# A decoder layer pair on one core: the last output product of the cross attention in two steps, the order of normalisations moved at three places, and the second block's rows loaded ahead of the second expert's weights

## The reference, cut to what matters

```python
x = x + L0_attn(layernorm(x))      # 32 heads of 64, 8 key heads, sinks
x = x + L0_xattn(layernorm(x), mask, ctx)   # 32 heads of width 16, 375 context rows
x = x + L0_ffn(layernorm(x))       # router, 8 experts, 2 per row: gelu(x Wg) * (x Wu), then Wd
x = x + L1_attn(layernorm(x))      # 16 heads of 128, low-rank keys and values
x = x + L1_xattn(layernorm(x), ctx, mask)
x = x + L1_ffn(layernorm(x))       # amplitude and phase, two rounds of products and layernorms
```

## Time and profile before

| | |
|---|---|
| three executions | 1752.63, 1756.43, 1756.64 us; median 1756.43 |
| the profiled execution, its own time | 1756.78 us |
| its span (first to last instruction) | 1754.5 us |
| TensorE busy / weight loads | 1700.0 us (97%) / 1137.6 us (65%) |
| VectorE, ScalarE, GpSimd busy | 986.4, 548.0, 458.5 us |
| mean granted TensorE clock | 0.996 |
| DMA | 172.26 MB, mean 98 GB/s |

### The profile page before, as it was taken

The page is one execution under the profiler, slowest core; times in us unless marked ns, Lnnn a source line. Parts: engine busy times, 40 slices in busy tenths (PEclk is TensorE's granted clock), DMA queues, the critical chain, the costliest instruction groups (busy, mean ns, idle before and its releaser), DMA issues.

```text
span 1754.5 us, 32913 instructions
## 1 busy us (share of the span) xinstructions
PE 1700.0 (97%) x13868; PEld 1137.6 (65%) x13868; DVE 986.4 (56%) x1901; ACT 548.0 (31%) x1515; POOL 458.5 (26%) x549
## 2 busy tenths in 40 slices
PE   7999999999999999999999999998999999999998
PEld 6876666657666666666546888877677775444444
DVE  3765556437777777677743111116554555664987
ACT  0343333524444444445410111110422222333411
POOL 2532323512222213222113000005231210002676
PEclk9999999999999999999989999999999999999999
DMA  9100012000000000000147988866000033752101
GB/s 394 49 1 1 1 43 73 1 27 19 13 8 19 4 17 20 8 13 1 67 171 294 347 334 335 335 231 229 2 1 1 1 137 129 241 189 84 29 14 42
DMA packets 31987, 172.26 MB, mean 98 GB/s; under 512 B 4024, under 2 KB 4024, under 8 KB 18176
## 3 DMA queue, kind: packets, MB, share of 16 engines
q1 hardware_dynamic: 29600, 162.82, 24.9%
q0 software_dynamic: 2240, 7.34, 1.2%
HBM read 155.46 MB, written 16.52 MB: 98 GB/s over the span
## 4 chain that ended last, share of the span: by engine, by line
PE 86%; DVE 10%; POOL 1%; issue 1%; ACT 1%; DMA 1%; POOLq 0%; DVEq 0%; ACTq 0%
PE PS L1312 9%; PE PS L1080 7%; PE PS L1131 6%; PE PS L1381 5%; PE PS L1459 5%; PE PS L1169 5%; PE PS L1490 4%; PE PS L1321 4%; PE PS L1426 4%; PE PS L1192 3%; PE PS L1209 3%; PE PS L1477 3%; PE PS L1139 3%; PE PS L1156 2%; PE PS L1161 2%; DVE R L1618 2%
## 5 line engine op out<-in xcount | busy, mean ns | idle before, releaser
L1312 PEld LDWEIGHTS PS<-R,W 128*128 128x128 f32 x1344 | 153.2, 192 | 11.7 <-issue 11.7
L1312 PE MATMUL PS<-R,W 128*128 128x128 f32 x1344 | 153.6, 275 | 2.2 <-DVE R L1811 2.2
L1634 DVE TENSOR_REDUCE nmw<-PS 112x2 f32<-112x750 f32 x128 | 114.1, 934 | 42.5 <-PE PS L1192 42.5
L2251 POOL TENSOR_TENSOR rstd<-veps,mhalf 128x1 f32<-128x1 f32 (+1 forms) x71 | 53.8, 757 | 307.2 <-DVE veps L1520 284.0
L1080 PE MATMUL PS<-xT,W 128*128 128x224 f32 x640 | 127.8, 360 | 1.0 <-ACT xT L2041 0.7
L1080 PEld LDWEIGHTS PS<-xT,W 128*128 128x128 f32 x640 | 122.2, 194 | 9.9 <-issue 7.6
L1818 DVE TENSOR_TENSOR R<-R,PS 128x512 f32<-128x512 f32 x21 | 14.5, 688 | 199.1 <-PE PS L1312 199.1
L1459 PE MATMUL PS<-W 128*128 128x512 f32 x256 | 119.8, 611 | 0.9 <-ACT R L2109 0.9
L2109 ACT ACTIVATE R<-PS 125x672 f32<-125x672 f32 x128 | 86.6, 730 | 85.8 <-PE PS L1209 85.8
L2277 POOL TENSOR_TENSOR R<-R 128x224 f32<-128x224 f32 x80 | 52.8, 661 | 223.4 <-DVE R L1545 116.6
L1381 PE MATMUL PS<-xT,W 128*128 128x224 f32 x512 | 101.9, 359 | 2.5 <-DVE R L1545 2.2
(11 more groups left out here) (306 smaller groups left out, 3325.3 us busy)
## 6 DMA issues: line engine op xcount, KB each, us to landing
W<-in_we SPq DMA_DIRECT2D x63, 1024.0 KB, 8.0
R<-in_ctxT SPq DMA_DIRECT2D x12, 750.0 KB, 7.3
W<-in_entwT SPq DMA_DIRECT2D x8, 1024.0 KB, 7.0
W<-in_entpw SPq DMA_DIRECT2D x8, 1024.0 KB, 8.3
R<-in_ctx SPq DMA_DIRECT2D x8, 750.0 KB
xs_rows<-in_x SPq DMA_DIRECT2D x3, 1792.0 KB, 36.1
R<-xs_rows SPq DMA_DIRECT2D x21, 256.0 KB, 8.3
ys_rows<-R SPq DMA_DIRECT2D x21, 256.0 KB, 8.5
```

Of the source, the lines that this page charges most:

```text
L1312: o = e.matmul(PS[:, m, c * 128:(c + 1) * 128], gate_up(j % 3, k, off + c * 128), BT[:, j % 2, k, :], start=k == 0, stop=k == 3)
L1634: e.tensor_reduce(nmw[0:S, par, :].rearrange("p (r f) -> p r f", r=4)[:, r:r + 2, 16 - 16 * par], PS[0:S, r:r + 2, 0:SC], AX.X, ALU.max, n ...
```

## The change

Some dozen of the 2210 steps change their place; no step is added, taken away or given another PSUM bank. The output product ("xw", 6) is cut in two on TensorE: three of its four products ask for less than the last.

```diff
@@ -382,7 +382,8 @@
                     k = fill.index(need)
                     mine = [f for f in fill[:k + 1] if f[0] == need[0] or {f[0], need[0]} in ({"ck", "ck1"}, {"pj", "rt"})]
                     out += [take(f) for f in mine]
-        out += runs[n]
+        final = n == 16 * NBATCH - 1
+        out += runs[n][:-1] + [("mt", *pieces_of(n // 4), 1)] + runs[n][-1:] if final else runs[n]
         due += unit * SHARE[n % 4]
         some = []
         while True:
@@ -390,11 +391,11 @@
             if not free or not (due > cost(free[0]) / 2 or n == 16 * NBATCH - 1 or n % 4 in MUST and not some):
                 break
             some.append(take(free[0]))
-        if n % 4 == 3:
+        if n % 4 == 3 and not final:
             some.insert(1, ("mt", *pieces_of(n // 4), 1))
         out += some
     h = part(range(5))
-    at_end = {("xk", 7, 3, 1): h[:1], ("xcv", 7, 3, 1): h[1:4], ("xd", 7, 3): [("scale", 2, 5)], ("xw", 6): h[4:5] + [("turn", 2, 5)] + h[5:6] + [("route", 1)]}
+    at_end = {("xk", 7, 3, 1): h[:1], ("xcv", 7, 3, 1): h[1:2], ("xw", 6): [("scale", 2, 5)] + h[2:3] + [("turn", 2, 5)] + h[3:4] + [("route", 1)]}
     for s in itertools.chain(*runs[16 * NBATCH:]):
         out += [s] + at_end.get(s, [])
     return out
@@ -402,9 +403,9 @@
 
 def experts():
 
-    out = [("load", "front", 3), ("load", "we", 0), ("load", "w1s", 0), ("scale", 2, 6), ("turn", 2, 6), ("route", 2), ("lt",)] + part([3]) + [("rank",)]
-    out += part(range(4, FRONT)) + [("ea", 0, k) for k in range(FRONT)] + [("put", t) for t in range(NT)]
-    out += [("load", "experts", 0), ("load", "rows", 0), ("load", "we", 1), ("load", "rows", 1), ("load", "rows", 2), ("load", "we", 2)]
+    out = [("load", "front", 3), ("load", "we", 0), ("load", "w1s", 0), ("scale", 2, 6), ("turn", 2, 6), ("route", 2), ("lt",)] + part([2]) + [("rank",)]
+    out += part(range(3, FRONT)) + [("ea", 0, k) for k in range(FRONT)] + [("put", t) for t in range(NT)]
+    out += [("load", "experts", 0), ("load", "rows", 0), ("load", "rows", 1), ("load", "we", 1), ("load", "rows", 2), ("load", "we", 2)]
     out += [("bt", 0), ("pc", 0), ("pc", 2)]
     for j in range(NBLK + 1):
         if j < NBLK:
@@ -458,6 +459,8 @@
 
 def pace1(step):
 
+    if step[0] in ("stats", "scale"):
+        return 0.0
     return float(step[0] == "d1") if step[0] in ("p1", "s1", "c1", "v1", "d1", "w1") else cost(step)
 
 
@@ -539,7 +542,7 @@
             if u == 0:
                 out += nxt[:4]
                 nxt = nxt[4:]
-            nxt = norms(0, bs) + nxt[:4] + turns(0, bs) + nxt[4:]
+            nxt = [("stats", 0, b) for b in bs] + nxt[:1] + [("scale", 0, bs[0])] + nxt[1:2] + [("scale", 0, b) for b in bs[1:]] + nxt[2:4] + turns(0, bs) + nxt[4:]
         else:
             nxt = norms(1, (0, 1)) + nxt[:4] + turns(1, (0, 1)) + norms(1, (2,)) + nxt[4:] + turns(1, (2,))
         if u == NU - 2:
@@ -563,7 +566,7 @@
         nxt = project1(u + 1) if u + 1 < NU else []
         if u + 2 < NU:
             bs = range(2 * u + 4, min(2 * u + 6, NT))
-            nxt = norms(3, bs) * (u > 0) + nxt[:5] + turns(3, bs) + nxt[5:]
+            nxt = nxt[:5] + turns(3, bs) + nxt[5:]
         if u + 1 < NU:
             nxt += [("bo1", t) for t in range(0 if u == 0 else 2 * u + 2, min(2 * u + 4, NT))]
         if u == NU - 1:
@@ -577,7 +580,11 @@
         if u == 0:
             second = attend1(1)
             out += norms(3, (4, 5)) + once[4:10] + second + once[10:]
-        out += spread([s for n in range(2 * (u == 0), 4) for s in attend1(4 * u + n)], nxt, pace1)
+        steps = [s for n in range(2 * (u == 0), 4) for s in attend1(4 * u + n)]
+        if u and u + 2 < NU:
+            k = steps.index(("c1", u, 0, 1)) + 1
+            steps[k:k] = norms(3, bs)
+        out += spread(steps, nxt, pace1)
     out += [("load", "c5", 0), ("load", "c5", 1), ("mu",)]
     out += attend1(4 * NU) + attend1(4 * NU + 1)
     out += [("load", "ent", 1, 0), ("load", "ent", 1, 3), ("load", "rows2a", 0)]
@@ -1260,9 +1267,12 @@
                     return
                 m = bank(("xw", t))
                 w.wait_ge(*at("d_q3", "wx"))
-                for b in (t, t + 1):
-                    w.wait_ge(*at("oxt", (b, 3)))
-                xw_part(t, m, range(4)).then_inc(*up("attended", ("xw", t)))
+                w.wait_ge(*at("oxt", (t, 3)))
+                if t == NT - 1:
+                    w.wait_ge(*at("oxt", (t + 1, 2)))
+                    xw_part(t, m, range(3))
+                w.wait_ge(*at("oxt", (t + 1, 3)))
+                xw_part(t, m, range(3 * (t == NT - 1), 4)).then_inc(*up("attended", ("xw", t)))
 
             def route(part):
                 m = bank(("route", part))
@@ -2326,9 +2336,9 @@
 
             def lt():
                 w.wait_ge(*at("var", 0))
+                e.tensor_tensor(rt[:, 8, 8:8 + NT], rt[:, 8, 0:NT], mhalf[:, 0:NT], ALU.pow).then_inc(*up("rms", 0))
                 for n in range(8):
                     e.memset(rsl(rt, 9)[:, :, n:n + 1], 8.0 - n).then_inc(*up("rank", n))
-                e.tensor_tensor(rt[:, 8, 8:8 + NT], rt[:, 8, 0:NT], mhalf[:, 0:NT], ALU.pow).then_inc(*up("rms", 0))
 
             def put(b):
                 w.wait_ge(*at("slot_no", 0))
```

## The result

The changed kernel takes **1745.57 us** (median of 4 executions, 1744.57 to 1749.1) against 1756.54 (4 executions, 1752.63 to 1757.42): a ratio of 0.9945, 95% interval 0.9925 to 0.9966. Later executions put the size in proportion: over all 15 of the changed kernel, these four among them, the median is 1747.05 (1743.9 to 1749.82), over 79 of the kernel before 1756.48, so about 9.4 us. Three later executions, of two of the experiments and of the kernel before, took 2439, 6053 and 7702 us and are left out of every figure.

What follows compares the result with a forecast made beforehand. The prediction took TensorE's own stream to bound the kernel (busy 1700.0 of 1754.5 us). Its terms, -1.30 - 0.82 - 3.05 - 2.37 + 0.1 = -7.4 us, took 1756.78 to 1749.3, range 1747.0 to 1753.6.

Steps and rivals of the forecast that it cites:

- scale(0,4) and (0,5) later: Layer 0: VectorE's copy comes before two scalings, so TensorE's value product no longer waits for it; gain 1.30 us.
- scale(0,6) frees no wait of TensorE: Layer 0: moving this third scaling later was to gain nothing, no TensorE wait being found there.
- cost nothing: Layer 0: the scalings' new places between rotations were to cost 0; 0.5 us for GpSimd contention went into the range.
- Gain 0.82: End of the cross attention: TensorE no longer waits for VectorE's addition of maxima, queued behind a denominator; 0.82 us.
- gain 3.05: End of the cross attention: with less idle time the clock stays up, so 6.1 us of work takes half the time.
- rival A: The clock falls all the same, or in another place: gain 4.4 us, time 1752.4; chance 0.2.
- xw(6): Output product split in two, less filler ahead: TensorE waits 0.1 us for the last piece, range 0 to 0.5.
- Rows 1: Expert stage: loading these rows ahead of expert 1's weights was to gain and cost nothing, only making a thin margin safe.
- rival C: Expert stage: the second expert's weights come late, with a 4.0 us wait at block 1; time 1760.3, chance 0.04.
- Layer 1, 2.37: Stats and scale (3,6) behind c1(1,0,1): two TensorE waits of 1.12 and 1.25 us go, gain 2.37.
- B: More half-clock time goes, such as the stretch from 910, or the start is kinder: 1747.8 us; chance 0.13.
- D: The change does little: waits pass to the next engine and the clock stays down, 1755.3 us; chance 0.08.

Runs made afterwards that it cites:

- mt alone: The kernel before with mt(7,3,1) moved ahead of xd(7,2) as its only edit: 1753.66 us, ratio 0.9982.
- The run with a wait of 2.50: The changed kernel, but xw(6) waits once for all four pieces before its first matmul: 1752.09 us, ratio 0.9968 to the kernel before.

## Why the prediction was right or wrong

*Direction and mechanisms* held. The median came out 3.7 below the forecast. Of that, 1.5 is luck: the first four executions were quick ones. Over all executions the waits gained 7.3, the clock 2.5; the prediction's terms say 4.4 and 3.05. **The miss is in the waits, and about half of it is the layer 0 term.**

*scale(0,4) and (0,5) later, "Gain 1.30"*: the step that failed, by its size. The stall was taken from the bracket in front of one group of matmuls, 1.30, while the product that held it ran from 71.82 to 75.74 instead of 1.65, with part of the stall inside groups that count as busy: 2.27. The 1.30 stands in the sum and in the clock argument too.

*"scale(0,6) frees no wait of TensorE, since I find none there: nothing"*: wrong, 1.1, for the same reason; shown by putting it back.

*"cost nothing" for the scalings' new places*: wrong by 0.54, about the 0.5 that the text kept for the range. The stretch that the row of 1.41 hinted at came, but on GpSimd's side: 1.77 beside a scaling for a multiplication that takes 1.32 without one, while the scaling kept its 0.54. GPSIMD Engine Reference, section "Key points", of the Trainium skill says that GpSimd shares its SBUF interfaces with VectorE, with contention for some of VectorE's instructions. The traces agree that the two engines get in each other's way, by 0.45 us here; which property of the scaling does it, no run shows. The term in all: -2.8 for -1.30.

*mt, "Gain 0.82"*: right (0.88 by starts in the trace, 0.9 at full clock with mt alone); the 0.88 and the 0.73 stayed as said.

*The clock, "gain 3.05"*: wrong in the changed kernel's first profile (rival A), where a fall still cost 1.7; right in its other two, and on average 2.3 at this place. What failed is only the either-or: the fall came in five of five profiles before and in two of nine after. Part came back near 1211 to 1224, where that window gives 0.74 (3.4 us) in both later profiles of the changed kernel, though 1.00 in its first, against 0.87 to 1.00 in the five with the old order; that the change does this is not shown. By TensorE: Matmul & The Clock Gate, section "HAM oscillation", of the Trainium skill, single long waits for transfers bring the clock down; its own case has waits of about 3 to 5 us. The run with a wait of 2.50, shorter and for VectorE, had a fall behind it and points the same way; the five falls of the old order, with no wait above 0.88 ahead, do not.

*xw(6), "0.1"*: 0.2. *Rank, nothing, up to 0.3*: nothing; the low clock behind the routing stayed, as expected, in all fourteen profiles. *"All gains pass"*: right, with the rows landed over 2 us ahead of the transpose. *Rows 1, "nothing"*: right; rival C did not show.

*Layer 1, 2.37*: 2.74 by starts in the trace of that part alone, the same reading of brackets, 0.4 short.

*The base.* The forecast stood on an execution at 1756.78, near the median, so that was no error; but the four executions of the changed kernel were quick ones by 1.5 us against its 15. Against the median of all, 1747.05, the forecast was 2.2 too high, and that is the layer 0 term (1.5) and layer 1 (0.4), less what the clock gave short (0.5), with 0.8 left over that no run assigns: parts one by one give 6.8 of the 7.3, each known to 0.3.

Rivals: A in one of three profiles of the changed kernel; B's 1747.8 is near where the kernel lands, but that is luck for B, since the stretch behind the routing stayed; C and D did not happen.

## What to carry to other kernels

Measure a stall on a pipelined engine from the start of one group to the start of the next, against the same group where nothing is late; the idle time in brackets gave 1.30 for 2.27, 1.4 for 2.34 and nothing for 1.10. When work is moved off a path, take it whole to a hole of the engine that does it (5 us here) instead of between two other deadlines: half moved, it won 1.5 of 2.3, and too late it made a wait of its own. Where executions differ by the clock, compare span times clock first, and count over several profiles how often a fall happens before putting a price on it. When a step moves, look at what it will stand beside on the other engines, too: a scaling of 0.54 stretched a neighbour by 0.45.

## What the runs showed of the hardware

The clock falls from run to run at different places for the same program: one changed kernel had a stretch at 884 in its first profile and none there in two others. With a wait of 0.82 us in a thin passage it fell in 5 of 5, without it in 2 of 9. A GpSimd multiplication of 112x448 took 1.77 us in the eight profiles in which VectorE scaled a 128x512 tile beside it, and 1.31 or 1.32 in the six in which it did not. A change of the clock's luck is worth as much as an edit: the executions of before spread over 8.5 us (1752.1 to 1760.65), while their full-clock mean was 1746.2, 1746.2 and 1746.1 on three chips.
